# Second attention stage: values, transposes and statistics take other places in the slot, and GpSimd makes the masked keys

## The reference

```python
x = x + tanh(g_xattn[0]) * attention0(layernorm(x), ctx)
x = x + tanh(g_ffn[0])   * experts(layernorm(x))
x = x + tanh(g_xattn[1]) * attention1(layernorm(x), ctx, mask)
x = x + tanh(g_ffn[1])   * quantised_ffn(layernorm(x))
# attention1, 16 heads of 16 numbers, one 128-token block at a time:
#   q = x wq + bq ; k = ctx wk + bk ; v = ctx wv + bv
#   p = softmax(q k' / 4 with -1e9 where mask == 0) ; out = (p v) wo + bo
```

## Time and profile before

| | us |
|---|---|
| median of 3 runs (lowest, highest) | 2046.25 (2039.37, 2049.42) |
| profiled execution, time | 2046.86 |
| profiled execution, span | 2045.0 |
| PE busy | 1735.7 (85%) |
| DVE busy | 1410.9 (69%) |
| ACT busy | 1156.4 (57%) |
| GpSimd busy | 567.4 (28%) |

### The profile page before, as it was taken

One profiled execution on the slowest core, in us unless ns is written; L12 is line 12 of the kernel. 1 busy time (PEld: TensorE's weight loads), 2 busy tenths in 40 slices (PEclk: granted clock), 3 DMA queues, 4 the chain that ended last, 5 costly groups with the idle time before them and its releaser, 6 DMA issues.

```text
span 2045.0 us, 53833 instructions
## 1 busy us (share of the span) xinstructions
PE 1735.7 (85%) x20198; PEld 1374.2 (67%) x20208; DVE 1410.9 (69%) x4649; ACT 1156.4 (57%) x2347; POOL 567.4 (28%) x551
## 2 busy tenths in 40 slices
PE   6999999999999994878888884888888888868855
PEld 4888888888888883667666663656666565643334
DVE  4788878888887874655444434677776767658988
ACT  3666666666666651222222224777777777758875
POOL 1000000000000002788888873111111111111147
PEclk9999999999999997989999997999999999989989
DMA  3112222222222225888888873211221222102255
GB/s 99 49 62 64 64 67 64 72 63 63 68 64 67 86 83 155 202 203 220 208 212 210 213 149 88 64 58 59 64 64 56 61 64 64 49 30 124 124 220 192
DMA packets 194481, 214.04 MB, mean 105 GB/s; under 512 B 25584, under 2 KB 170352, under 8 KB 192048
## 3 DMA queue, kind: packets, MB, share of 16 engines
q1 hardware_dynamic: 169408, 171.97, 26.0%
q0 software_dynamic: 24816, 38.62, 10.4%
HBM read 125.63 MB, written 84.89 MB: 103 GB/s over the span
## 4 chain that ended last, share of the span: by engine, by line
PE 62%; DVE 21%; DMA 6%; issue 6%; POOL 3%; ACT 1%; SPq 1%; POOLq 0%; DVEq 0%; ACTq 0%
DVE mt L825 8%; PE tiles L378 7%; PE tiles L361 7%; PE bank L408 6%; PE bank L444 6%; PE bank L524 6%; DMA xr<-token_rows,tid 4%; PE bank L487 4%; PE bank L1280 3%; PE bank L476 3%; PE bank L456 3%; PE tiles L1312 3%; PE bank L547 3%; PE tiles L345 2%; DVE hmax L1702 2%
## 5 line engine op out<-in xcount | busy, mean ns | idle before, releaser
L1961 POOL TENSOR_TENSOR rstd<-var,minus_half 128x2 f32<-128x2 f32 x138 | 96.3, 698 | 1119.7 <-DVE var L902 1119.5
L825 DVE TENSOR_REDUCE mt<-tiles 128x16 f32<-128x2048 f32 x128 | 293.5, 2293 | 114.8 <-PE tiles L361 114.8
L608 ACT ACTIVATE pt<-tiles 128x2048 f32<-128x2048 f32 x128 | 240.8, 1881 | 35.6 <-PE tiles L378 35.6
L1489 POOL DMA_INDIRECT accumulator<-ye,tid x128 | 206.7, 1615 | 47.3 <-issue 30.1
L1434 DVE TENSOR_SCALAR ye<-bank,xr 128x256 f32<-128x256 f32 x128 | 56.0, 479 | 197.7 <-PE bank L1324 195.4
L1474 POOL DMA_INDIRECT xr<-token_rows,tid x128 | 140.8, 1100 | 69.6 <-DVE within L1402 32.6
L444 PE MATMUL bank<-xt,w_q 128*128 128x128 f32 x1024 | 154.1, 284 | 0.9 <-ACT xt L616 0.9
L378 PE MATMUL tiles<-qm,qkp 32*128 32x128 f32 x4096 | 152.0, 285 | 0.9 <-DVE mt L825 0.9
L361 PE MATMUL tiles<-qkp 32*128 32x256 f32 x2048 | 148.0, 401 | 3.5 <-ACT qkp L633 3.4
L444 PEld LDWEIGHTS bank<-xt,w_q 128*128 128x128 f32 x1024 | 131.0, 194 | 22.5 <-issue 20.2
L378 PEld LDWEIGHTS tiles<-qm,qkp 32*128 32x128 f32 x4096 | 127.4, 188 | 27.1 <-issue 24.6
(11 more groups left out here) (246 smaller groups left out, 4059.3 us busy)
## 6 DMA issues: line engine op xcount, KB each, us to landing
keys_values<-res SPq DMA_DIRECT2D x64, 256.0 KB, 3.0
cxax<-accumulator SPq DMA_DIRECT2D x128, 128.0 KB, 2.3
cxax<-keys_values SPq DMA_DIRECT2D x128, 128.0 KB, 2.5
hidden_away<-h_ring SPq DMA_DIRECT2D x8, 1536.0 KB, 5.1
token_rows<-pay SPq DMA_DIRECT2D x64, 160.0 KB, 1.8
pt<-in_expert_up SPq DMA_DIRECT2D x36, 256.0 KB, 3.9
cxax<-in_ctx SPq DMA_DIRECT2D x64, 128.0 KB, 2.3
res<-in_x SPq DMA_DIRECT2D x64, 128.0 KB, 2.3
```

The source lines that it names most:

```text
L608: nc.scalar.activation(pt[r % 2][:, :, :], tiles[:, :, :], ACT.Exp).then_inc(sem("exp_done"), 1)
L825: nc.vector.tensor_reduce(mt[:, :].rearrange("p (i n c) -> p i n c", i=RT, n=2 * KC)[:, :, :, 0], tiles[:, :, :].rearrange("p i (n k) -> p ...
L1489: nc.gpsimd.indirect_dma_start(out=acc[p][:, :], out_offset=bass.IndirectOffsetOnAxis(ap=tid[b % 8][:, h:h + 1], axis=0), in_=ye[r][:, h, ...
```

## The change

On each engine the slot of the second attention gets another order, and some steps take a block that is one slot older. PE: `values` handles o instead of k and stands right behind `scores`, and `transposes` stands before `scores_t`. ACT: `copy_v` first, `normalise_second` for u, `copy_ov` for o, and `copy_xt` before the exponent. DVE: the variances, the first half of norming and `token_maximum` (for u) move ahead of `head_sums`; the variances pair with v; they get a wait for the step before. `PAIR[1]` becomes 7. The four masked copies of the keys are made by GpSimd as `tensor_scalar` operations in its loop over the blocks, behind the power; `scores` waits for them (`keys_masked`), and SP's load of the next keys does too.

```diff
-        PAIR = (4, 6)
+        PAIR = (4, 7)
@@ scores
                 if L == 1:
                     masks(0)
+                    pe.wait_ge(sem("keys_masked"), b + 1)
@@ PE body
                 else:
+                    values(o)
                     project_qk(f)
+                    transposes(g)
                     scores_t(k)
                     heads_to_tokens(o)
                     output(w)
                     tokens_to_heads(o)
-                    transposes(g)
                     maxima_t(m)
-                    values(k)
@@ copy_qk
-                if L == 1:
-                    act.wait_ge(sem(f"kv_in{p}"), 16 * (b - p) + 32)
...
-                    k = bank[5][:, (KC + j) * P:(KC + j + 1) * P] if L == 0 else kvt[p][:, j * P:(j + 1) * P]
-                    for e in range(2):
-                        last = nc.scalar.activation(kp[r][:, e, j, :], k, ACT.Identity, bias=kb[:, e, j:j + 1], scale=keep[:, e:e + 1])
+                    for e in range(2 * (1 - L)):
+                        last = nc.scalar.activation(kp[r][:, e, j, :], bank[5][:, (KC + j) * P:(KC + j + 1) * P], ACT.Identity,
+                                                    bias=kb[:, e, j:j + 1], scale=keep[:, e:e + 1])
@@ ACT body
-                    normalise_second(v)
+                    copy_v(f)
+                    normalise_second(u)
                     normalise_first(g)
+                    copy_ov(o)
                     copy_qk(f)
-                    copy_v(f)
+                    copy_xt(g)
                     exponent(k)
                     copy_at(o)
-                    copy_xt(g)
-                    copy_ov(k)
@@ variances
+                if L == 1 and (n is not None or k is not None):
+                    wait(dve, sm("rstd_step"), NORM_STEPS * (n[0] if n is not None else k[0] + PAIR[L]))
@@ DVE body
-                y = o if L == 0 else w
+                y = o if L == 0 else v
...
                     first_stats(n)
+                    variances(n, y)
+                    norming(1)
+                    token_maximum(u)
                     head_sums(o)
                     head_norm(o)
-                    token_maximum(v)
-                    residual(y)
-                    second_stats(y)
-                    variances(n, y)
-                    norming(1)
+                    residual(w)
+                    second_stats(w)
                     shifted(m)
                     norming(1)
@@ SP load_keys_values
-                wait(sp, sm("qk_out"), 2 * (b - 1))
+                wait(sp, "keys_masked", b - 1)
@@ GpSimd
+            def mask_keys(b):
+                r, p = b % 4, b % 2
+                pool.wait_ge(sem(f"kv_in{p}"), 16 * (b - p) + 32)
+                wait(pool, "st_done", NB + b - 3)
+                for j in range(KC):
+                    for e in range(2):
+                        last = G.tensor_scalar(kp[r][:, e, j, :], kvt[p][:, j * P:(j + 1) * P], keep[:, e:e + 1], kb[:, e, j:j + 1],
+                                               ALU.mult, ALU.add)
+                last.then_inc(sem("keys_masked"), 1)
+
             for s in range(NB + PAIR[1]):
                 inverse_roots(pool, 1, s)
+                if 1 <= s <= NB:
+                    mask_keys(s - 1)
```

More of the change, by code:

```diff
@@ L1039, in body @@
             def body(stage):
-                m, o, w, v = (stage(lag) for lag in (1, 3, 4, 5))
+                m, o, w, v, u = (stage(lag) for lag in (1, 3, 4, 5, 6))
                 n = stage(-1 if L == 0 else -2)
                 r = route(v if L == 0 else None)
-                y = o if L == 0 else w
+                y = o if L == 0 else v
                 q = inverses(n, y)
@@ L1928, in _ @@
             sp.wait_ge(sem("qk_out_1"), 2 * NB)
+            sp.wait_ge(sem("keys_masked"), NB)
             sp.wait_ge(sem("v_out_1"), NB)
```

## The result

| | before | after |
|---|---|---|
| median of the runs, us | 2043.7 (4 runs) | 1976.0 (4 runs) |
| ratio to before | 1 | 0.966, 95% interval 0.963 to 0.970 |
| profiled execution, us | 2046.9 | 1975.5 |
| its span, us | 2045.0 | 1973.6 |

The forecast was 1980, the range 1966 to 2004. Every execution behind these and the later medians lies within 1% of its kernel's median, except one of the six of the kernel with maxima_t in bank 5, which took 9335 us for a reason that is not on record; without it that median is 1953.5.

A forecast was written before the change was run, and what follows sets the result against it. Instruction order, not a full engine, was taken to set the 8.92 us slot; 1.07 us saved in 60 blocks (64) plus 3 for the fill and 0 for the drain gave 67 us, 2046.3 to 1979, forecast 1980, range 1966 to 2004.

The forecast's parts named there:

- The chain: Waits within one second-attention slot, maximum to maximum: values between maxima_t and the masks holds 1.01 us; slot 8.92 to 7.85.
- PE's load: PE from the start of the masks through transposes: 3.70 us against 3.93 available, so it fits at cost 0.
- Values left the path: values moved behind scores, one slot later: its 1.01 us leave the path and lie under the maximum.
- A: Rival: PE or DVE late in the new slot, queue gaps make it 8.05 to 8.35 us, time 2000; chance 0.16.
- D: Rival: residual does not hold maxima_t and the exponent's loop bounds: slot 7.48 us, time 1954; chance 0.05.
- The mask on GpSimd: Key masks moved from ACT to GpSimd: 0.35 us each, four make 1.4 us, lying in a hole of GpSimd's work.
- The fill: Start of the second attention stage, before residual is active: a gain of 3 us.
- the exponent's loop: Slot's other loop, through the exponent: 7.48 us, the bound only in the two full slots before residual is active.
- The drain: End of the second attention stage: chain kept, one link longer in slots but not in work; 0, within 2 us.
- The 60 slots: Blocks after the first four in the second attention: 1.07 us gained in each, 64 us.
- would end at about 2.6: ACT's copies in the new order with four key masks kept there: they end at 2.6 and push the exponent.
- B: Rival: port shared by DVE and GpSimd, each block waits for one 0.35 us mask, slot 8.2, time 2000; chance 0.11.

The follow-up runs named there:

- the kernel with sixteen: Changed kernel with twelve more tensor_scalar operations per block on GpSimd, sixteen masks in all, into memory nobody reads: 2025 us, ratio 0.989 to the kernel before.

## Why the prediction was right

The chain was read rightly, and its points can be laid beside the new slot (times after the maximum's end at 1498.38): residual forecast 3.09, measured 3.09; maxima_t 3.71 and 3.72; masks 3.96 and 3.96; exponent's start 1.67 and 1.67; nmr's end 5.1 and 5.0; slot 7.85 and 7.82. PE's load from the masks to the end of transposes was forecast 3.70; the transposes at 1497.96 start 3.44 us after the masks of that slot, which by its length of 7.82 began at 1494.52 (1502.34 less 7.82), so with about 0.25 for them it is 3.69, and PE has the 0.2 us of room I gave it. Values left the path for 1.01 us forecast and 1.05 measured by putting it back. A did not happen: PE is 95% busy (380 of 400 us) and the slot is still 7.82. D is refuted as a reading and confirmed as a bound: residual does hold maxima_t, and where it doesn't, the slot is 7.47, within 0.01 of the 7.48 that D gave.

Three terms were mis-sized. The mask on GpSimd took 448 ns, not 350; the cover made that harmless. The fill was to give 3 us and gave 0.5. The slot between the second and third maximum took 8.6 us where I had the exponent's loop at 7.5, and the clock was at 0.50 from 1265 to 1270 us. The kernel with the new order alone has the same order of PE, and there the clock stayed at 1.00:

```profile
1255.00:1275.00 20.00, 14.60 (x275) 10.27 (x275) 13.69 (x27) 14.69 (x32) 4.67 (x7) 1.00 0.35 106
```

The slot between the same two maxima took 7.47 us there, and 7.47 as well in the kernel with bank 5 and DVE's part undone, whose masks are on GpSimd and whose clock was at 1.00 too. So the loop was read rightly, and the 1.2 us on top go with the lower clock. From its first mask product to its fourth maximum the kernel with the new order alone saves 1.9 us. What makes the clock fall in one execution and not in the other, these runs don't show. The drain was to give 0 and gave 3.5: about 2.4 because the lower clock fell there in the profiled execution before, and about 1.1 by the order, as shown above. The 60 slots gave 65.7 us where I had 64. That the whole came out so near is in part luck: the medians differ by 67.7 us where I had 67, but the two profiled executions differ by 71.4, of which 3.0 lie behind the stage and 2.4 are the clock's in the drain, while 1.2 were lost to it in the fill.

The sentence that with the masks on ACT the copies "would end at about 2.6" was wrong: the exponent starts at 2.08 there (1508.11 less 1506.03), because I summed mean durations of overlapping operations. The conclusion drawn from it, that the move buys the room for the reordering, is true only by 0.065 us in this kernel.

B did not happen. The residual takes 484 ns in the changed kernel against 474 before, but it takes 484 as well in the kernel whose masks are on ACT, so this isn't GpSimd's doing. It goes with DVE's order: with that part undone and the masks still on GpSimd it takes 473. There, as before, it follows token_maximum directly, and in the new order it begins after a short idle time (7.7 us over 51 of them, in the rows above).

A better kernel follows from the reading: maxima_t in bank 5 takes 1954 us, 1.1% under the changed one, and it needs DVE's order and the masks on GpSimd, each worth 0.4 us a slot there. What values in its old place would cost in that kernel was not measured.

## What to carry to other kernels

Find the loop that sets the slot, write down each step's start to start, and move the one instruction on it that nobody in the loop waits for; here, with one step of 1.01 us put back, the whole gain of 3.4% was gone. Work out the next loop's length as well, since it says what other edits are worth: moving the masks, worth 0.065 us a slot, and DVE's new order, worth 0.1, became worth 0.4 each when the first loop was shortened. For the load of an engine sum start-to-start distances and not mean durations; and look for a buffer shared by two unrelated steps, since its wait looks like a data dependence.

## What the runs showed that I had not expected

A tensor_scalar of 128x128 float32 with two per-partition scalars takes 448 ns on GpSimd, 435 start to start, and sixteen in a row take 7.09 us, 443 each (1499.56 to 1506.65 in the kernel with sixteen). On ACT the same operation has a mean of 483 ns, but a pair of them takes 0.86 or 0.87 us. PE's granted clock is not the same from execution to execution at the same place: behind the same idle time of 2.42 us under the last maximum it was at the lower level in the kernel before (scores_t 2.09 us) and at the upper one in the kernel with the key masks alone (1.17 us). Two profiled executions can differ by 2.4 us through that alone.
